# Attention heads of a two-block transformer kernel: queries projected beside the keys, back-transposes in the value bank, scores at the end of PE's step, maxima and exponentials taken in pairs

## The reference

```
h = layernorm(x)*(1+ca)+sa ; x = x + ga * linear_attention_and_mlp(h)   # block 0
h = layernorm(x)*(1+cb)+sb ; x = x + gb * sum over 8 experts of (silu(h Wg) * (h Wu)) Wd
h = layernorm(x)*(1+ca)+sa ; x = x + ga * causal_attention_8_heads(h)   # block 1
h = layernorm(x)*(1+cb)+sb ; x = x + gb * attention_16_heads(h)
```

```
q = x Wq ; k = x Wk ; mix_v = top-2 gates (sigmoid) of x Ws ; v = mix_v combined with x Wv over 8 experts
probs = softmax(q k^T / 8)            # 512 x 512 for each of 16 heads
attn = probs v
mask_o = top-2 of x Wd ; result = sum over heads, experts of mask_o * (attn Wo)
```

## Time and profile before

| | |
|---|---|
| median of 3 runs | 3109.82 us (3106.86 to 3110.35) |
| the profiled execution | 3113.69 us, of which the profile's span is 3111.7 us |
| busy share of the span | PE 82%, DVE 50%, ACT 44%, POOL 26% |
| mean granted TensorE clock | 0.915 of full speed |

### The profile page before, as it was taken

The page is one execution under the profiler, slowest core; times in us unless marked ns, Lnnn a source line. Parts: engine busy times, 40 slices in busy tenths (PEclk is TensorE's granted clock), DMA queues, the critical chain, the costliest instruction groups (busy, mean ns, idle before and its releaser), DMA issues. The chain is left out here.

```text
span 3111.7 us, 43916 instructions
## 1 busy us (share of the span) xinstructions
PE 2559.5 (82%) x14892; PEld 1579.8 (51%) x14892; DVE 1570.6 (50%) x2650; ACT 1367.7 (44%) x2945; POOL 806.4 (26%) x370
## 2 busy tenths in 40 slices
PE   4884699879897898879897898988988798986476
PEld 2353346554475445655365544754456544664254
DVE  4235753546635384454735465354834457336622
ACT  0232226553364525553364524555255533653254
POOL 1002620105501181013701064012800137004500
PEclk6896799989898998999999898989989899998699
DMA  2110010102001120012101020011200121001001
GB/s 73 41 48 8 10 51 1 55 15 72 16 15 41 41 59 2 15 55 55 33 7 49 14 76 12 15 41 41 59 2 15 55 55 32 15 14 39 1 28 31
DMA packets 210733, 101.59 MB, mean 33 GB/s; under 512 B 137367, under 2 KB 189620, under 8 KB 210492
## 3 DMA queue, kind: packets, MB, share of 16 engines
q1 hardware_dynamic: 205052, 95.74, 11.1%
q10 hardware_dynamic: 5440, 2.75, 0.3%
HBM read 77.48 MB, written 20.99 MB: 32 GB/s over the span
## 5 line engine op out<-in xcount | busy, mean ns | idle before, releaser
L690 POOL TENSOR_TENSOR prod<-pv,mixv 128x1024 f32<-128x1024 f32 x184 | 598.8, 3294 | 270.2 <-ACT pv L1133 163.2
L1510 DVE TENSOR_REDUCE nmax<-bank 128x1 f32<-128x512 f32 x512 | 341.3, 686 | 629.5 <-PE bank L972 628.1
L1169 ACT ACTIVATE prT<-bank 128x512 f32<-128x512 f32 x512 | 305.7, 597 | 615.6 <-PE bank L705 610.7
L972 PE MATMUL bank<-keys,qs 64*128 64x512 f32 x1024 | 324.5, 712 | 218.1 <-ACT pr L1182 99.0
L629 POOL TENSOR_TENSOR rstd<-vareps,minus_half 128x4 f32<-128x4 f32 x48 | 50.1, 1043 | 1511.6 <-DVE vareps L1279 1511.5
L1182 ACT ACTIVATE pr<-bank,nmax 128x512 f32<-128x512 f32 x512 | 349.7, 685 | 161.4 <-DVE nmax L1510 160.3
L705 PE MATMUL bank<-ident,pr 128*128 128x128 f32 x2048 | 362.9, 304 | 27.5 <-ACT prT L1169 27.5
L705 PEld LDWEIGHTS bank<-ident,pr 128*128 128x128 f32 x2048 | 246.6, 153 | 253.5 <-issue 201.9
L1075 ACT ACTIVATE arena<-bank 128x512 f32<-128x512 f32 x256 | 152.9, 597 | 461.9 <-PE bank L817 384.8
L1008 PE MATMUL bank<-prT,vals 128*64 128x128 f32 x4096 | 289.3, 285 | 40.1 <-ACT prT L1169 40.1
L1475 DVE TENSOR_REDUCE vals<-prod 128x128 f32<-128x1024 f32 x256 | 305.2, 1207 | 32.8 <-POOL prod L690 32.8
(11 more groups left out here) (220 smaller groups left out, 3188.2 us busy)
## 6 DMA issues: line engine op xcount, KB each, us to landing
Wg<-in_L_ffn_Wg SPq DMA_DIRECT2D x64, 256.0 KB, 2.7
Wu<-in_L_ffn_Wu SPq DMA_DIRECT2D x64, 256.0 KB, 3.1
Wd<-in_L_ffn_Wd SPq DMA_DIRECT2D x64, 256.0 KB, 3.8
out_rows<-on SPq DMA_DIRECT2D x32, 512.0 KB, 2.6
onR<-out_rows SPq DMA_DIRECT2D x32, 512.0 KB, 3.9
xin<-in_L_attn_x SPq DMA_DIRECT2D x8, 256.0 KB, 4.3
mask_rows<-masko SPq DMA_DIRECT2D x8, 256.0 KB, 4.3
maskR<-mask_rows SPq DMA_DIRECT2D x8, 256.0 KB, 6.9
```

What stands on the lines that cost most here:

```text
L690: g.tensor_tensor(*value_piece(n), ALU.mult).then_inc(vprod_r[0], 1)
L972: pe.matmul((S0, S1)[(turn + odd) % 2][:, :], qs[half, j % 3, r, :], keys[half, p, :], start=True, stop=True).then_inc(s_ps[0], 1)
L1169: s.activation(prT[:, m % 3, :], TB[:, :], ACT.Copy).then_inc(pT_r[0], 1)
L1510: v.tensor_reduce(nmax[:, m % 2:m % 2 + 1], (S0, S1)[turn % 2][:, :], X_AXIS, ALU.max, negate=True).then_inc(nmax_r[0], 1)
```

## The change

**Queries.** They are no longer steps. `qs` holds a whole sequence (eight pairs by 512 tokens). In `values`, PE projects a pair of query heads for all 512 tokens (one 128x512 matmul into OB) where n % 4 is 1, and the keys go to TB alone where n % 4 is 3; ACT copies each at the same mark. The stage `begin` is gone.

**Steps.** There are 64 head steps and 16 behind them. Mixed and result are extras at the start of a step. PE's step k is now: the extra, transposes of k - 2, value product of the pair k - 4 and k - 3, back, and the scores of k and k + 1 last. ACT's step is: the extra's copy, `prT` of k - 2, `oaT`, then both exponentials of k and k + 1. DVE takes both maxima at the even step.

**Back.** It transposes into OB, the bank of the value product, and the value product behind it waits for `on`.

**Buffers.** `pr` and `nmax` have 4 parts where they had 2.

The core of the diff:

```
-QUERIES_AT = (4, 8)
-BACK_AT = (14, 6)
-MIXED_AT = 10
+MIXED_AT = (6, 8)
 RESULT_AT = 12
+BUILD_AT = 2
+NPR = 4
+NPRT = 3
...
+for i in range(NT):
+    EXTRA[HS * (i + 1) + MIXED_AT[0] + 2 * (i == NT - 1)] = ("mixed", 2 * i)
+    EXTRA[HS * (i + 1) + MIXED_AT[1] + 2 * (i == NT - 1)] = ("mixed", 2 * i + 1)
+    EXTRA[HS * (i + 1) + RESULT_AT] = ("result", i)
...
@@ PE, values @@
+                    if n % 4 == 1:
+                        p = n // 4
+                        if p == 0:
+                            wait(pe, hdB_r, b, 1)
+                            wait(pe, pv_r, b, 2)
+                        else:
+                            wait(pe, q_r, b, p)
+                        pe.matmul(OB[:, :], WqT[:, p * P:(p + 1) * P], hdB[:, :], start=True, stop=True).then_inc(q_ps[0], 1)
...
@@ PE, steps, behind mixed and result @@
+                    m = k - 2
+                    if 0 <= m < N2:
+                        wait(pe, s_out, b, head_out(m))
                         if m >= 1:
                             wait(pe, pT_r, b, m)
-                        transposes(TB, lambda j: pr[:, m % 2, j * P:(j + 1) * P]).then_inc(p_T[0], 1)
+                        transposes(TB, lambda j: pr[:, m % NPR, j * P:(j + 1) * P]).then_inc(p_T[0], 1)
+                    m = k - 4
+                    if 0 <= m < N2 and m % 2 == 0:
...
+                        if h % GROUP == 0 and m:
                             wait(pe, oa_r, b, m // GROUP)
+                            if h % (HS // 2) == 0:
+                                wait(pe, on_r, b, m // (HS // 2))
+                        wait(pe, pT_r, b, m + 2)
...
+                    if 0 <= m < N2 and m % (HS // 2) == HS // 2 - 1:
+                        half = m // (HS // 2)
+                        wait(pe, oa_r, b, 2 * (half + 1))
+                        for p in range(NP // 2):
+                            last = pe.transpose(OB[:, p * P:(p + 1) * P], oaT[:, NP // 2 * (half % 2) + p, :], ident[:, :])
+                        last.then_inc(back_ps[0], 1)
+                    if k < N2 and k % 2 == 0:
+                        i, p = k // HS, k % HS // 2
+                        for odd in range(2):
+                            turn = head_turn(k + odd)
+                            free(b, turn)
+                            half = slice(DS * odd, DS * odd + DS)
+                            pe.matmul((S0, S1)[turn % 2][:, :], qs[half, p, i * P:(i + 1) * P], keys[half, p, :], start=True, stop=True).then_inc(s_ps[0], 1)
...
@@ ACT, steps @@
+                    m = k - 2
+                    if 0 <= m < N2:
+                        wait(s, p_T, b, m + 1)
+                        s.activation(prT[:, m % NPRT, :], TB[:, :], ACT.Copy).then_inc(pT_r[0], 1)
...
+                    if k < N2 and k % 2 == 0:
...
+                        for odd in range(2):
...
+                            wait(s, nmax_r, b, m + 1)
...
+                            s.activation(pr[:, m % NPR, :], (S0, S1)[turn % 2][:, :], ACT.Exp, bias=nmax[:, m % NPR:m % NPR + 1], accum_out=den[:, i % 2, h + odd:h + odd + 1]).then_inc(s_out[0], 1)
```

More of the change, by code:

```diff
@@ L92 @@
-HEAD_STEPS, FINISH_AT = head_steps()
-STEP_AT = {step: k for k, step in enumerate(HEAD_STEPS) if step[0] != "rest"}
-TURN = [sum(kind != "rest" for kind, _ in HEAD_STEPS[:k + 1]) for k in range(len(HEAD_STEPS))]
-NTURNS = TURN[-1]
-COPIED = [sum(kind not in ("rest", "result", "back") for kind, _ in HEAD_STEPS[:k + 1]) for k in range(len(HEAD_STEPS))]
-NCOPIED = COPIED[-1]
-BUILD_AT = {STEP_AT["mixed", 2 * i] - BUILD_BEFORE: i for i in range(NT)}
-MARKS["begin"] = BEGIN = 2
-MARKS["heads"] = FINISH_AT - BEGIN
@@ L104 @@
-CLOSE_AT = STEP_AT["mixed", 2 * (NT - 1)]
-MARKS["finish"] = (CLOSE_AT - FINISH_AT + 1) // 2
-MARKS["close"] = len(HEAD_STEPS) + 1 - CLOSE_AT
-CLOSE_BEHIND, BEGIN_BEHIND = 4, 28
+NSTEPS = N2 + 16
+FINISH_AT, CLOSE_AT = N2, N2 + 8
+EXTRA = {}
+for i in range(NT):
+    EXTRA[HS * (i + 1) + MIXED_AT[0] + 2 * (i == NT - 1)] = ("mixed", 2 * i)
+    EXTRA[HS * (i + 1) + MIXED_AT[1] + 2 * (i == NT - 1)] = ("mixed", 2 * i + 1)
+    EXTRA[HS * (i + 1) + RESULT_AT] = ("result", i)
+EXTRA_AT = {extra: k for k, extra in EXTRA.items()}
@@ new lines, with head_turn, extra_turn, head_out @@
+EXTRAS_BY = [sum(j <= k for j in EXTRA) for k in range(NSTEPS)]
+MIXED_BY = [sum(j <= k and EXTRA[j][0] == "mixed" for j in EXTRA) for k in range(NSTEPS)]
+NTURNS, NCOPIED = N2 + 3 * NT, N2 + 2 * NT
+def head_turn(m):
+    return m + 1 + EXTRAS_BY[m - m % 2]
+def extra_turn(k):
+    return min(k, N2) + EXTRAS_BY[k]
+def head_out(m):
+    return m + 1 + MIXED_BY[m - m % 2]
+def mixed_out(x):
+    k = EXTRA_AT["mixed", x]
+    return min(k, N2) + MIXED_BY[k]
+TURNS = {head_turn(m): ("head", m) for m in range(N2)} | {extra_turn(k): extra for k, extra in EXTRA.items()}
@@ L110, in weight @@
+assert sorted(TURNS) == list(range(1, NTURNS + 1))
+MARKS["heads"] = FINISH_AT
+MARKS["finish"] = (CLOSE_AT - FINISH_AT) // 2
+MARKS["close"] = NSTEPS - CLOSE_AT
+CLOSE_BEHIND = 4
 def weight(name, m):
@@ L935, in close @@
             def close(b):
-                yield from steps(b, CLOSE_AT, len(HEAD_STEPS) + 1)
+                yield from steps(b, CLOSE_AT, NSTEPS)
             def free(b, turn):
                 if turn > 2:
-                    before = TURN.index(turn - 2)
-                    what, y = HEAD_STEPS[before]
-                    if what == "result":
-                        wait(pe, xout_r, b, y + 1)
-                    elif what == "back":
-                        wait(pe, on_r, b, y + 1)
+                    kind, x = TURNS[turn - 2]
+                    if kind == "result":
+                        wait(pe, xout_r, b, x + 1)
@@ L947, in free @@
                     else:
-                        wait(pe, s_out, b, COPIED[before])
+                        wait(pe, s_out, b, head_out(x) if kind == "head" else mixed_out(x))
             def steps(b, first, end):
                 for k in range(first, end):
-                    kind, x, turn = step_of(k)
-                    bank_k = (S0, S1)[turn % 2]
-                    if kind == "head":
-                        for odd in range(0 if x % 2 else 2):
-                            free(b, turn + odd)
-                    elif kind != "rest":
-                        free(b, turn)
@@ L973, in steps @@
-                    if kind == "back":
-                        wait(pe, oa_r, b, NBACK * (x + 1))
-                        for p in range(NJ):
-                            last = pe.transpose(bank_k[:, p * P:(p + 1) * P], oaT[:, NJ * (x % 2) + p, :], ident[:, :])
-                        last.then_inc(s_ps[0], 1)
+                    kind, x = EXTRA.get(k, ("", 0))
+                    if kind:
+                        turn = extra_turn(k)
+                        bank_k = (S0, S1)[turn % 2]
+                        free(b, turn)
```

199 lines of the change are left out of this document (79 added, 120 removed).

## The result

The changed kernel takes 3337.67 us (median of 4 runs, 3333.28 to 3347.22), the kernel before 3108.34 us beside it (4 runs, 3096.47 to 3110.35). The ratio is 1.0751, with a 95% interval of 1.0724 to 1.0779: slower, as forecast, but by 229 us where I had +45, and far outside my range.

The account below looks back on a forecast made before the run. PE, busy 82% of the span, was taken as the bound. The profiled 3113.7 + 29 (lone heads and around) + 16 (six turns) + 0 (sequence 6's heads) = 3158.7, less 3.9 for the median: 3155 us, range 3075 to 3215.

Parts of the forecast that it names:

- The chain of a lone pair: Lone heads, scores to next scores: 5.4 us a pair after the change, PE idle 2.15 us; -1 us in all.
- The mixed step: Lone heads: mixed comes too early for its DMAs; each of three tiles loses 2.7 us, +8 in all.
- The clock in the lone heads: Lone heads: holes in each pair bring half clock; +20 us, a quarter of the pairs, ends 0 and +42.
- I take 70% in series: 108 + 34 = 142, no change: Heads beside gates and front: 70% of PE's 49 us of other work adds to the 108 us chain.
- The third piece of the heads: Last 142.1 us of a turn's heads, beside gates and front: 0, ends -34 and +15; clock +3 us.
- The first two pieces: Heads beside the small attention's projections and scores: fewer query steps save 1 us and 3 us a turn.
- The experts: Loop's experts stage: eight query matmuls more, two query steps fewer, one expert mark; +3.6 us a turn, ends 0 and +9.
- Table loads: Loop: two activation table loads fewer a turn, 12 in all, 1.28 us each; taken as 0, end -15 us.
- Sequence 6 and behind it: Last sequence's heads 0 us (ends -15, +15); its values behind on +1, two transposes in a row in the tail +1.
- 56% in series: Heads beside gates and front: share of PE's other work in series from which the change gains, -7 us a turn.
- the front fills the holes: Heads beside gates and front: 35% of 49 us in series, 125 us a turn, 3088 us in all; chance 0.28.
- the clock collapses: Half of the lone pairs at half clock and 8 us a turn in the loop: 3207 us; chance 0.07.

Follow-up runs that it names:

- filler: The changed kernel with three unused 128x512 matmuls more in each pair of the lone heads: 3320.1 us.
- scores_first: The changed kernel with PE's scores of a pair moved right behind the extra, ahead of transposes and value product: 3114.9 us.
- before_queries: The kernel before with only the query part of the change (no query steps, qs for a whole sequence): 3148.8 us.
- close_half: The changed kernel with the eight steps of close in four marks of the weaving in place of eight: 3294.3 us.
- first_later2_close: The changed kernel with scores moved ahead of transposes, three tiles' mixed steps two pairs later, on waiting for onR's DMA, close in four marks: 2960.8 us.

## Why the direction was right and the size wrong

**The chain of a lone pair** was right: 5.4 us forecast, 5.55 measured, with the idle time of 2.25 us (forecast 2.15) ended by the copy, and back in the hole at no cost (5.60 us).

**The mixed step** was right in kind and small in size. I gave each of three tiles 2.7 us; its pair takes 10.3 to 12.1 in place of 5.55 us. The wait itself came at the forecast place, but PE ran at half clock behind it. In all, undoing it gave 28 us, of which my sum had 8.

**The clock in the lone heads** was sized well: +20 forecast, about 17 by filler. The Trainium skill ("TensorE: Matmul & The Clock Gate", "A second HAM failure mode: psum-queue depth-cycling") says that short idles between groups make the clock swing at a cost in throughput. The trace agrees in kind (0.82 for 0.97, holes of 2.25 us in each pair); the upper end of +42 us, which I would have taken by it, did not come. The quarter that I took was a choice between 0 and +42, so that it fits so closely is in part luck.

**The failed step: "I take 70% in series: 108 + 34 = 142, no change".** The third piece of the heads took 156.9 us. With my own 108 us of chain and 49 us of other work in PE that is all of it in series, as in my upper end of +15. In fact it is more than all, for PE had less to do there: one mixed step (32 records, 2.3 us) and 24 records of `attn1` (3.4 us) now stand in the second piece. On like work the third piece is some 20 us longer (an estimate), where the sum had 0, and 3 for the clock. All of the front in series makes 15 of these. The granted clock fell from 0.94 to 0.89, 18 us more of half clock, and that is where I would look for the rest; no run separates the two. The largest waits of PE in that piece:

```profile
PE bank L701 <- ACT prT L1169: 11.5, 6, 2.2
PE bank L963 <- DMA onR<-out_rows: 6.5, 2, 4.3
PE bank L990 <- DVE on L1509: 4.5, 2, 2.3
PE bank L701 <- DVE nrm_o L1280: 3.8, 2, 1.9
```

The waits of the heads' own lines add up to about 24 us there, as before the change (26 us). Those of the front's lines (`nrm_o`, `h1T`, `arena`, `kv`, `att`) add up to 17 us, for 3 us before: nearly all of the added idle time stands ahead of the front's instructions. So the reason that I gave for 70% (the front's steps hang on ACT and DVE instructions) fits nearly all of them. That these stand behind both exponentials or maxima is argued from the queues' order. Over the loop the heads, from first scores to the experts, take 1591 us for 1485, that is +106 where my sum had -6, and scores_first brings them to 1453.

**The first two pieces**: forecast -4, measured +1.1 and +2.8 us. The second piece has the 5.7 us of work from the third; without it, it is near the -3 of my sum (an estimate). But before_queries, where the same query steps go from the heads and nothing else does, shows no gain: its heads take 1494 us in the loop for 1485, as the waits for exponentials grew.

**The experts** were forecast at +3.6 us a turn, by the query matmuls and one expert mark. Measured is +6.3 us up to the last `Wg` and 2 to 3 us more until the heads begin. The query matmuls are 2.6 us of it (before_queries), and the five to eight marks of `close` most of the rest (close_half).

**Table loads**: 12 fewer, as said, 45 to 33 for the two lines of the earlier trace rows. What they are worth was not measured. The Trainium skill's 2.66 us for a switch ("ScalarE: Activation LUTs", "What ACT_TABLE_LOAD costs") would have given up to 32 us; no run here separates it from the rest. The trace agrees with the page on the load itself (1283 ns).

**Sequence 6 and behind it**: forecast 0 and +2, measured 16 us without its experts: 12 in its heads, and 4 in the values behind it, the gap to the second lone scores and the end. Its heads have the same holes as the third piece, and I should have treated them so.

By spans the change cost 221 us: 106 in the heads of the loop where I had -6, 56 in the experts up to the next scores where I had 22, 45 in the lone heads where I had 27, 16 for the rest where I had 2, and 2 less ahead of the loop. Of my signs, the chain, the waiting mixed step and the lone clock under 0.9 came true; the third piece within 10 us of 142 and the experts 3 to 5 us longer did not. The 56% in series from which the change would have been a gain was far off. My rival "the front fills the holes" also had a slip: the 29 and 16 of the sum are already in 3155, so by its own terms it gives 3155 - 102 - 10 = 3043 us and not 3088. The sum by the page's price of the switches is 3123, not 3121. The rival "the clock collapses" was nearest in time, but for another reason: by filler, clock is 17 of the 45 us in the lone heads.

What stays open: why scores_first in the changed kernel is worth 223 us when the pair effect on the kernel before is 90; how much of the loop's loss is half clock; why before_queries loses 43 us; and what queries and back in OB earn in first_later2_close, where they were not undone.

## What to carry to other kernels

When a queue's order is changed, write out the whole cycle through all queues, and mark what stands behind a wait that it doesn't need: here a copy of 0.6 us behind two exponentials, with a value product behind it, turned two edits worth 0 and -27 us into a loss of 62 us on the kernel before, and in the changed kernel moving one block of two matmuls took 223 us back. For the work of another stage that is to fill holes, count what is ready at that time in program order; without evidence take all of it in series. Where a schedule is woven by numbers of marks, a stage cut into more marks delays all that comes behind it, even if it has no more work.

## What the runs showed of the hardware

More matmuls made a program faster: 93 more (186 records), three in each of 31 pairs of the lone heads, took 18 us off the whole, with the granted clock at 0.99 for 0.82 of full speed, that is 2.4 GHz nearly throughout for a mix with 1.2 GHz. PE had been busy 70% of that stretch with one hole of 2.25 us in each pair, and most pairs of the same instructions took from 5.55 to 7.4 us, those with a mixed step aside.

The two score matmuls of a pair use 64 partitions each, and the trace shows them side by side. In the changed kernel their first records start 0.01 us apart (3187.88 and 3187.89) and all four records end after 1.13 us. In first_later2_close the second bank comes free later: the second matmul starts 0.67 us behind the first, and the four records take 1.79 us. No idle time shows between them, since the first matmul alone takes 1.12 us. So the 87% of the span that PE is busy in first_later2_close holds such waits.
